# Moving the projections that stand behind the last product of a step to in front of it

## What is computed

```python
qk    = relu(bn(conv1x1(x, qk_w)))            # 256 channels
val   = relu(bn(conv1x1(x, v_w)))             # 512 channels
key, value = psp(qk), psp(val).T              # max-pooled cells: 1+9+36+64 = 110 per image
s     = softmax(qk.T @ key * 256**-0.5)       # every position against 110 cells
y     = s @ value
out   = x + bn(conv1x1(y, out_w))
```

## Time and profile before

| | us |
|---|---|
| median of three timed runs | 1304.71 (1304.1 to 1305.56) |
| the profiled execution | 1303.7 |
| its span in the trace | 1302.0 |
| TensorE (PE) busy | 1282.8 |
| GpSimd (POOL) busy | 952.4 |
| VectorE (DVE) busy | 947.3 |
| ScalarE (ACT) busy | 688.4 |

### The profile page before, as it was taken

The page is one execution under the profiler, slowest core; times in us unless marked ns, Lnnn a source line. Parts: engine busy times, 40 slices in busy tenths (PEclk is TensorE's granted clock), DMA queues, the critical chain, the costliest instruction groups (busy, mean ns, idle before and its releaser), DMA issues.

```text
span 1302.0 us, 16831 instructions
## 1 busy us (share of the span) xinstructions
PE 1282.8 (99%) x5561; PEld 1037.5 (80%) x5561; DVE 947.3 (73%) x2171; ACT 688.4 (53%) x1017; POOL 952.4 (73%) x414
## 2 busy tenths in 40 slices
PE   9999999999999999999999999999999999999997
PEld 7777788887888878887888878888788887888885
DVE  6555677777777778778677787777768778786576
ACT  5333565654555654556644566644555637764422
POOL 2888988877787867878777887877878835765532
PEclk9999999999999999999999999999999999999999
DMA  6323356567676656676567675666666669995426
GB/s 227 113 97 114 113 187 217 189 216 226 210 240 218 199 192 232 213 242 210 173 224 234 211 245 190 198 217 234 210 226 213 202 216 351 326 339 185 156 98 259
DMA packets 134537, 272.20 MB, mean 209 GB/s; under 512 B 9226, under 2 KB 9266, under 8 KB 134450
## 3 DMA queue, kind: packets, MB, share of 16 engines
q1 hardware_dynamic: 134162, 270.59, 61.8%
q10 hardware_dynamic: 288, 0.52, 0.1%
HBM read 174.61 MB, written 96.47 MB: 208 GB/s over the span
## 4 chain that ended last, share of the span: by engine, by line
PE 81%; POOL 7%; DVE 6%; ACT 3%; issue 2%; DMA 1%; DVEq 0%; SPq 0%; ACTq 0%; POOLq 0%
PE conv_ps L700 17%; PE conv_ps L698 17%; PE conv_ps L702 17%; POOL xl L582 5%; PE out_ps L793 4%; PE out_ps L794 4%; PE out_ps L795 4%; PE conv_ps L682 3%; PE conv_ps L683 3%; PE conv_ps L684 3%; PE score_ps L756 2%; PE score_ps L755 2%; PE score_ps L757 2%; DVE row_max L1366 1%; PE sum_ps L765 1%
## 5 line engine op out<-in xcount | busy, mean ns | idle before, releaser
L1366 DVE TENSOR_REDUCE row_max<-conv_ps 128x64 f32<-128x384 f32 (+2 forms) x576 | 284.8, 530 | 139.8 <-ACT q_out L1059 68.4
L582 POOL TENSOR_TENSOR xl<-xa,xh 128x1024 fp32r<-128x1024 f32 x108 | 258.0, 2416 | 81.7 <-ACT xh L988 81.5
L698 PE MATMUL conv_ps<-xh,sh 128*128 128x512 f32 x648 | 253.4, 391 | 3.8 <-POOL xl L582 1.9
L700 PE MATMUL conv_ps<-xh,sl 128*128 128x512 f32 x648 | 254.4, 393 | 0.0
L702 PE MATMUL conv_ps<-xl,sh 128*128 128x512 f32 x648 | 254.3, 392 | 0.0
L582 POOL TENSOR_TENSOR xl<-tt,xh 128x1024 fp32r<-128x1024 f32 x81 | 194.2, 2414 | 10.7 <-ACT xh L988 10.7
L698 PE MATMUL conv_ps<-xh,wh 128*128 128x512 f32 x486 | 190.0, 391 | 3.8 <-POOL xl L582 2.7
L702 PE MATMUL conv_ps<-xl,wh 128*128 128x512 f32 x486 | 190.7, 392 | 0.0
L700 PE MATMUL conv_ps<-xh,wl 128*128 128x512 f32 x486 | 190.6, 392 | 0.0
L1506 DVE SCALAR_TENSOR_TENSOR xo<-out_ps,shift,xo 128x512 f32<-128x512 f32 x205 | 151.9, 745 | 42.7 <-DMA xo<-x 26.5
L996 ACT ACTIVATE conv_ps<-conv_ps 128x512 f32<-128x512 f32 x81 | 47.2, 583 | 253.2 <-PE conv_ps L702 252.4
(11 more groups left out here) (245 smaller groups left out, 2528.2 us busy)
## 6 DMA issues: line engine op xcount, KB each, us to landing
xa<-x SPq DMA_DIRECT2D x148, 512.0 KB, 5.6
xo<-x SPq DMA_DIRECT2D x104, 512.0 KB, 4.3
out<-xo SPq DMA_DIRECT2D x104, 512.0 KB, 3.8
queries<-q_out SPq DMA_DIRECT2D x112, 256.0 KB, 2.5
q_in<-queries SPq DMA_DIRECT2D x50, 512.0 KB, 4.1
tt<-x SPq DMA_DIRECT2D x13, 512.0 KB, 5.6
out<-tt SPq DMA_DIRECT2D x13, 512.0 KB, 4.6
early<-queries SPq DMA_DIRECT2D x6, 512.0 KB, 8.2
```

What stands on the lines that cost most here:

```text
L582: nc.gpsimd.tensor_tensor(xl[:, b0:b1, :], raw, xh[:, b0:b1, :], ALU.subtract).then_inc(x_lo, 1)
L698: nc.tensor.matmul(out[:, :], hi[:, k, :], xh[:, b + k, :], start=first, stop=False, skip_group_check=True)
L700: nc.tensor.matmul(out[:, :], lo[:, k, :], xh[:, b + k, :], start=False, stop=False, skip_group_check=True)
L1366: last = nc.vector.tensor_reduce(row_max[:, c, n, :], src[:, r0_ * W:r1_ * W].rearrange("p (r w) -> p w r", w=W), AX.X, ALU.max)
```

## The change

In ordinary pairs, in the first call (j = 0) `project(B0, 0)` moves from behind P4 into the third fill, behind `project(A - 2, 3)` and in front of P4; in the third call (j = 2) `project(A, 1)` moves in the same way behind `project(A, 0)`. The fourth fill of both is empty. The second call, pairs in which an image ends, the tail, and the orders of the other engines stay.

```diff
                     pair_product(s, 0,
                                  lambda: sums_of(B0),
                                  lambda: projections((A - 2, 2)),
-                                 lambda: projections((A - 2, 3)),
-                                 lambda: projections((B0, 0)))
+                                 lambda: projections((A - 2, 3), (B0, 0)),
+                                 nothing)
...
                     pair_product(s, 2,
                                  lambda: projections((B0, 3)),
                                  lambda: scores_of(A + 1),
-                                 lambda: projections((A, 0)),
-                                 lambda: projections((A, 1)))
+                                 lambda: projections((A, 0), (A, 1)),
+                                 nothing)
```

## The result

The changed kernel takes 1307.55 us (median of 15 runs, 1306.45 to 1309.75), the kernel before 1304.52 in the 15 runs beside them: ratio 1.0024, 95% interval 1.0017 to 1.0032. That is 3.1 us more at 1304.5. The sum of the prediction was +3.4, its time 1308.1. The interval is 2.2 to 4.2 us: that the kernel is slower is clear, and whether by more than the 2.6 us that the prediction set as its bound is not.

A forecast was written before the change was run, and what follows sets the result against it. TensorE, busy 99% of the span, was taken as the bound. Terms 0 + 0 + 3.2 + 0.2 gave +3.4 us: 1307.1 on the profile's 1303.7, and 1308.1 with the median 1.0 higher; range 1305.5 to 1309.6.

The forecast's parts named there:

- No idle time to win in ordinary pairs: Ordinary pairs, the only ones edited: TensorE is busy for all of 153.10 us, so a better order gains nothing.
- moved projections don't stall: Both moved projections, started 1.38 us earlier: operands and banks are ready, the first with 1.6 us to spare; cost 0.
- First call: cost 0: First call, P4 0.70 us later: VectorE's reduction ends at 541.89, still ahead of its residual wait to 542.67; cost 0.
- Third call, into an ordinary pair: absorbed: 12 pairs: VectorE's 0.67 us idle for ScalarE's reciprocal guess absorbs the 0.64 us delay; cost 0, 0.7 us left.
- Third call, into a pair in which an image ends: 5 x 0.64 = 3.2: Pairs 8, 12, 16, 20, 24: ScalarE's late split delays VectorE's chain to make_u7 and P4; 0.64 us each, 3.2 us.
- The loss of P3: Pairs where an image ends: P3 may lose 0.1 to 0.2 us to make_u4, inside the make_u7 wait, costing nothing more.
- Tail: 0.2, between 0 and 0.4: Tail: row (2, 3) shifts 0.70 us, partly absorbed before TensorE's wait at 1086.68; cost 0 to 0.4, taken as 0.2.
- The sum: Whole kernel: 0 + 0 + 3.2 + 0.2 = +3.4 us, giving a time of 1308.1.
- rival D: 36 places, fewer target bank changes at P4: faster, 1302, needing 0.07 to 0.17 us each; gain put at about 0; chance 0.03.
- The signs: Pairs where an image ends: five P4 waits 0.9 us, row (2, 3) 1.86 us after P1, period 157.0 us.
- B: Third call: the delay doesn't arrive through ScalarE and VectorE; 1304.7 to 1305.5, or 1306.5 with half; chance 0.12.
- C: More pairs stall, P3 in 12 ordinary pairs, 1309 to 1312, or the clock halves at P4, 1315; chance 0.07.

The follow-up runs named there:

- experiment 1: Kernel before with only the first call's projection moved, in all 18 ordinary pairs: 1303.56 us against 1304.05, ratio 0.9991.
- experiment 2: Kernel before with only the third call's projection moved, in all 18 ordinary pairs: 1307.06 us, ratio 1.0021 to the kernel before.
- experiment 3: Changed kernel, but third call as before in pairs 7, 11, 15, 19, 23 and 27: 1303.47 us, ratio 0.9990 to the kernel before.
- experiment 4: Changed kernel with ScalarE storing a pair's last query row ahead of its split of part 6: 1302.44 us, ratio 0.9983 to the kernel before.
- experiment 5: Changed kernel with the next pair's two sums matmuls also before P4 in pairs 7, 11, 15, 19, 23: 1308.99 us against 1304.09 before.
- experiment 6: Changed kernel with VectorE's addition of block 2 put behind make_u7 in pairs where an image ends: 1307.71 us, ratio 1.0026 to the kernel before.

## Why the prediction was right

- **No idle time to win in ordinary pairs; moved projections don't stall.** Right: that stretch has TensorE busy for all of 153.10 us again, and no kernel of experiments 1 to 4 has a new wait in an ordinary pair's first or third call.
- **First call: cost 0.** Right (experiment 1), with a gain of 0.02 us per moved projection that the steps lack.
- **Third call, into an ordinary pair: absorbed.** Right. The idle time of 0.67 us ahead of `refine` in pair 14 is 0.18 in the changed kernel, and TensorE has no wait:

```profile
534.62 0.70 DVE L1480 SCALAR_TENSOR_TENSOR sum_ps<-sum_ps,r 128x512 f32<-128x512 f32 x1 [0.18 <-ACT r L1115]
```
- **Third call, into a pair in which an image ends: 5 x 0.64 = 3.2.** Right in mechanism and place (experiments 3, 4, 5), 0.70 each in size, the upper of the bounds that the prediction gave ("no slack at all"). The 0.06 is the slack I gave ScalarE: it started its split 0.10 us after P4's last matmul ended (607.64), not the 0.04 I took from another row. It had started 0.10 us after it before as well (604.79 and 604.89). The loss of P3 is inside the 0.70, as said.
- **Tail: 0.2, between 0 and 0.4.** Right: the projection that was at 1086.68 comes 0.17 us later, counted from the start of the tail. All five kernels in which pair 27's third call has the move have it at 12.27 to 12.29 us, the five without it at 12.12. The wait itself grew by only 0.05 us (0.32 to 0.37); the other 0.12 or so is a late start 2 us ahead of it.
- **The sum.** 3.5 + 0.17 - 0.7 = 3.0 us for the change itself, against 3.0 by the medians and 3.1 by the ratio. The forecast of +3.4 was near because the gain of 0.7 that it lacked was partly offset by 0.3 too little at the five places; that part is luck. The gain is the term it put at about 0, under rival D, from two starts 0.23 us apart.
- **The signs.** P4's five waits are 0.8 us, foretold 0.9; row (2, 3) is at 1.92 us behind P1, foretold 1.86; the period is 156.95 to 157.16 us, foretold 157.0. The growth is in the pair in which the image ends, as foretold, but the ordinary pairs shrink.
- **The rivals.** B fell with experiments 2 and 3: the delay arrives in full. C: no ordinary pair stalls, and the clock stays at 1.00 (2.4 GHz) in the stretch with the 0.98 us of lateness; no run here has a longer wait in this part, so what the rule of the Trainium skill (TensorE: Matmul & The Clock Gate, "HAM oscillation — how this bites in real kernels") would do beyond that is not shown. D has its sign from experiment 1, but 0.02 us a place and not the 0.07 to 0.17 that it needed.

What is open: where the 0.02 us per moved projection comes from. It is there in each kernel that has the move and only in the call that is edited. The traces say where to look: in a product's matmuls the ten intervals behind a projection are 0.232 us on average, and from the eleventh on they are 0.227 (22 places in the trace of the kernel before). The move puts two projections together, so that a call has one such stretch fewer. Fewer switches between projections and products is then the idea at hand; nothing here tests it.

## What to carry to other kernels

On an engine that never waits, moving work "out of the way" can win nothing; ask whose input the moved-back instruction is. Follow its signal through each in-order queue to the next place where the signal's receiver has no idle time, and count the places where that holds: here 5 of the 18 moved projections of the third call cost 0.70 us each and the one in front of the tail 0.17; the other 12 cost nothing. When a queue holds both a long instruction that can wait and a short one that others want, both ready at the same signal, put the short one first; that one line took 4.9 us off the changed kernel by the traces, more than the 3.5 us that the change had cost in those places.

A delay or a gain that is seen at one wait need not stay there (experiments 5 and 6). Measure the whole stretch between two fixed instructions, not the wait.

## What the runs showed of the hardware

A late start costs more than its own wait: the next matmul starts 0.30 to 0.34 us after it, not 0.23 (618.69 and 619.00 at P4 of pair 16). So even a wait that ends almost in time (P3 at 614.18, 0.06 us late, the next at 614.49) costs 0.14 us. I had counted that only where a wait was visible before.

A matmul that waits for VectorE started 0.14 to 0.15 us behind the end of VectorE's instruction (615.70 and 615.84 before, 618.54 and 618.69 after). ScalarE's split started 0.10 us behind the end of P4's last matmul (607.64 and 607.74), its store 0.04 us (606.38 and 606.42 in experiment 4).
